# Lookups and pairwise products of a recommendation tower: 16-bit ids, 36 matmuls instead of 40 in a turn, and operands issued in another order

## The chip, the cores and the metric

The kernel runs on one core of a Trainium2 chip. The metric is the device time of one execution in microseconds, as the median of several executions. TensorE is called PE here, VectorE DVE, ScalarE ACT, GpSimd POOL, and SP is the engine that only issues transfers.

## The reference, cut to what matters

```python
def reference(r_bottom_output, ids, tbl_0, ..., tbl_25, W_top1, b_top1, W_top2, b_top2, W_top3):
    e = jnp.stack([tbl_0[ids[:, 0]], tbl_1[ids[:, 1]], ..., tbl_25[ids[:, 25]]], axis=1)   # (512, 26, 128)
    all_emb = jnp.concatenate([r_bottom_output[:, None, :], e], axis=1)                    # (512, 27, 128)
    gram = jnp.einsum('bfd,bgd->bfg', all_emb, all_emb)
    z = gram[:, _TRIU_I, _TRIU_J]                    # the 351 pairs f < g of each sample
    h = jnp.concatenate([z, r_bottom_output], axis=1)                                      # (512, 479)
    h = jnp.maximum(h @ W_top1 + b_top1, 0.0)        # (512, 512)
    h = jnp.maximum(h @ W_top2 + b_top2, 0.0)        # (512, 256)
    return h @ W_top3                                # (512, 1)
```

Everything is fp32. The batch has 512 samples. Nine of the 26 tables have 1000 rows and are looked up in another way than the rest.

## The kernel before, in words

Each engine has its own program, written out by hand in one block, and semaphores tie the programs together. There is no scheduler: the order in the source is the order on the engine.

**Lookups.** Nine tables of 1000 rows (`LOOKED_UP`) are multiplied by one-hot matrices. SP loads a whole table into `tab` (a ring of 3) and the ids of that feature for all 512 samples, broadcast over the partitions, into `hot`. DVE subtracts the first row number of each partition (L351), and makes most of the eight one-hot tiles of 125 x 512 with `is_equal` (L356, `dve_tiles`). ACT makes the rest in two steps, a square (L430) and a relu (L434): one tile in even lookups and two in odd ones. ACT rounds the table to `tab_hi` (L424), DVE subtracts to get `tab_lo` (L297), and PE multiplies both by the one-hots, 8 matmuls each of 512 columns (L661, L666). ACT copies the result into `embT` (L485).

**Gathers.** The other 17 tables are read row by row. POOL issues one indirect DMA for each table and each tile of 128 samples, 68 in all (L284), into `emb`. It starts when `idx`, the ids in sample order, has landed (`s_ids`). The gathered rows are grouped in five banks for each tile (`BANKS`, four features each and one in the last). PE transposes a bank (L535) after its gathers have landed (`s_row[t][i]`) and after an earlier bank has left the same PSUM buffer. Even banks are copied into `embT` by DVE (L294), odd ones by ACT (L412). For tiles 2 and 3 a gather also waits until PE has read the buffer that it overwrites.

**Products.** For each of four tiles of 128 samples, `gram` makes the products of all pairs with 256 small matmuls in the program, in two halves (L549). ACT and DVE copy the halves to `rows` (L217). `turn` (L564) brings them with selection matrices into the layout `products`: for each of four groups of samples it runs over `TURNS`, eight matmuls of three columns of features and two short ones for the last pairs. Then come the layers: high and low parts of the products (L447, L297), layer 1 (L573, L574, L581), relu (L462), transposes of the hidden layer (L622), their high parts (L469) and low parts (L297), and layer 2 and 3 for that tile. The PE program interleaves these stages of neighbouring tiles. The fp32 matmuls of gram and turn appear in the trace as two matmuls each, with a weight load before each of them: 1024 for L549 and 320 for L564.

Two places are touched at the start. SP issues `idx`, waits until it has landed, and then issues the first table's parts, the bottom rows `bot`, the next ids and tables. ACT waits for `s_ids` too before it issues `hot` for the first lookup (L472).

```python
            sp.dma_start(idx[:, :], ids.rearrange("(p t) f -> p (t f)", t=TILES)).then_inc(s_ids, 16)

            sp.wait_ge(s_ids, 16)
            load_table(0, 0, VP_MAIN, 0, VK // 2, s_tab[0])
...
            act.wait_ge(s_ids, 16)
            act.dma_start(hot[:, 0, :], hot_ids[0:1, :].broadcast_to([128, B])).then_inc(s_hotids[0], 16)
```

Of the kernel before, what the change touches and what calls it, by code (L numbers as in the profile page):

```python
# [21 lines left out]
B = 512  # L22
D = 128
TABLES = 26
FEATURES = TABLES + 1
TILES = B // 128
# [4 lines left out]
KTILES = 3  # L31
# [3 lines left out]
         for n in range(8)] + [(range(1, 3), 0, 1, 0, 31), (range(2, 3), 1, 1, 1, 31)]  # L35
LAST_TURN = {j: n for n, (_, _, _, j, _) in enumerate(TURNS)}
# [19 lines left out]
def dve_tiles(i):  # L56

    return VK - 1 - i % 2
# [10 lines left out]
def tower(nc, bottom, ids, hot_ids, tables, w1, w2, b2, w3, out):  # L69
    fp32, fp32r, i32 = mybir.dt.float32, mybir.dt.float32r, mybir.dt.int32  # L70
# [3 lines left out]
    with ctx:  # L74
# [10 lines left out]
        hot = sb("hot", [128, RING, B], i32)  # L85
# [15 lines left out]
        sel = sb("sel", [128, len(TURNS), 4, 32])  # L101
# [126 lines left out]
        def _(sp):  # L228
# [12 lines left out]
            def load_weights(c):  # L241
                sp.wait_ge(s_look, (LOOKED - RING + c // 2 + 1) * VK)
                if c <= KTILES:
                    dst, src = chunk(c), w1[:, c, :]
                else:
                    dst = chunk(c).rearrange("p (k n) -> p k n", n=N2)
                    src = w2.rearrange("(k p) n -> p k n", p=128)[:, 2 * (c - KTILES - 1):2 * (c - KTILES), :]
                sp.dma_start(dst, src).then_inc(s_w[c], 16)

            sp.dma_start(idx[:, :], ids.rearrange("(p t) f -> p (t f)", t=TILES)).then_inc(s_ids, 16)  # L250

            sp.wait_ge(s_ids, 16)
            load_table(0, 0, VP_MAIN, 0, VK // 2, s_tab[0])
            load_table(0, VP_MAIN, VP, 0, VK, s_tab[0])
            load_table(0, 0, VP_MAIN, VK // 2, VK, s_tab0_rest)
            sp.dma_start(bot[:, :, :], bottom.rearrange("(p t) d -> p t d", t=TILES)).then_inc(s_bot, 16)
            load_lookup(1)
# [32 lines left out]
        def _(dve):  # L290
# [49 lines left out]
            nc.vector.memset(sel[:, :, :, :], 0.0).then_inc(s_sel0, 1)  # L340
            dve.wait_ge(s_row0, 1)
            nc.vector.tensor_copy(row0f[:, :], row0[:, :]).then_inc(s_row0f, 1)
            dve.wait_ge(s_sel0, 1)
            dve.wait_ge(s_ident, 1)
            for n, (_, feature, features, j, row) in enumerate(TURNS):
                nc.vector.tensor_copy(sel[:, n, :, row:row + features], ident[:, :].rearrange(
                    "r (s f) -> r s f", f=32)[:, :, feature:feature + features]).then_inc(s_sel, 1)
            dve.wait_ge(s_row0f, 1)
            for i in range(LOOKED):
# [14 lines left out]
                if 2 <= i < 2 + len(BANKS):  # L364
                    copy_bank(0, i - 2)
            low_weights(0, FIRST_CHUNKS)
            for i in range(LOOKED - 2, len(BANKS)):
                copy_bank(0, i)
            copy_bank(1, 1)
            dve.wait_ge(s_bothi, 1)  # L370
            subtract(bot_lo[:, :, :], embT[:, :, :, 0], bot_hi[:, :, :]).then_inc(s_botlo, 1)
# [36 lines left out]
        def _(act):  # L408
# [62 lines left out]
            act.wait_ge(s_ids, 16)  # L471
# [4 lines left out]
            for i in range(LOOKED):  # L476
# [4 lines left out]
                if i == 0:  # L481
# [5 lines left out]
                if 0 < i <= len(BANKS):  # L487
                    copy_bank(0, i - 1)
# [22 lines left out]
            high_products(2)  # L511
            relu(2)
            copy_bank(3, 2)
# [11 lines left out]
        def _(pe):  # L525
# [29 lines left out]
            def turn(t):  # L555
# [28 lines left out]
            def layer1_bottom(t):  # L584
                if t == 0:
                    pe.wait_ge(s_wlo, 1)
                    pe.wait_ge(s_bothi, 1)
                    pe.wait_ge(s_botlo, 1)
                else:
                    pe.wait_ge(s_h1, 2 * t)  # L590
                for psum, cols in h1_parts(t):
# [60 lines left out]
            for i in range(LOOKED):  # L652
# [15 lines left out]
                if i == 0:  # L668
# [5 lines left out]
                elif i <= len(BANKS):  # L674
                    transpose_bank(0, i - 1)
# [114 lines left out]
```

## Time and profile before

| | us |
|---|---|
| median of 3 runs | 115.28 (115.25 to 115.95) |
| the profiled execution's own time | 115.62 |
| its span in the profile | 113.8 |
| PE busy | 92.2 (81% of the span) |
| POOL busy, nearly all of it the issue of gathers | 69.8 (61%) |
| DVE busy | 65.2 (57%) |
| ACT busy | 61.9 (54%) |

The span is the time between the first and the last recorded instruction; 1.8 us of the execution's own time lie around it. The profiled execution took 0.34 us longer than the median. The busy shares are averages over three stages: lookups until about 51 us, then the four tiles, then the tail of the last tile after about 95 us. "Idle ... <-issue" in a row means that the engine waited for nothing that the profile shows.

### The profile page before, as it was taken

Reading aid. Unit: us, or ns where it says so; the run is one execution under the profiler, and the core shown is the slowest. Engines: PE = TensorE matmul, PEld = TensorE weight load, DVE = VectorE, ACT = ScalarE, POOL = GpSimd, SP = SyncE. Lnnn points to the kernel's source line nnn. Section 1 sums busy time; section 2 is a strip of 40 time slices with the busy share of each in tenths; the row PEclk is TensorE's granted clock in tenths of the full one; section 3 lists DMA queues with packets and bytes.
Section 4 is the critical chain, followed back from the end, with each engine's and each line's share of the span. In section 5 each row is a group of like instructions: output and inputs, shape, how many; then the busy total and the mean of one; then the engine's idle time right before and its main releaser. Section 6 shows DMA issues by size and latency. Waiting matters only on the chain.

```text
span 113.8 us, 3965 instructions
## 1 busy us (share of the span) xinstructions
PE 92.2 (81%) x1692; PEld 73.8 (65%) x1692; DVE 65.2 (57%) x166; ACT 61.9 (54%) x90; POOL 69.8 (61%) x75
## 2 busy tenths in 40 slices
PE   0008999998999797997566999999999995886891
PEld 0007776876776584886445867888786884765771
DVE  6429997999999999964924081416303245120221
ACT  0626499999999999979702234254414145100330
POOL 2777777777777777777777777677777730000000
PEclk9999999999999999999998599999999999999999
DMA  0599989999788887367121222122212210000000
GB/s 19 146 312 281 281 185 242 194 245 227 189 256 215 198 261 228 86 232 233 48 53 46 63 58 56 48 52 69 52 46 61 66 46 0 6 6 6 3 0 1
DMA packets 6701, 13.70 MB, mean 120 GB/s; under 512 B 1926, under 2 KB 2567, under 8 KB 6684
## 3 DMA queue, kind: packets, MB, share of 16 engines
q1 hardware_dynamic: 4364, 8.73, 27.8%
q0 software_dynamic: 2176, 4.46, 15.8%
q10 hardware_dynamic: 144, 0.26, 1.0%
q8 instruction: 13, 0.21, 0.8%
q14 instruction: 4, 0.03, 0.1%
HBM read 13.44 MB, written 0.00 MB: 118 GB/s over the span
## 4 chain that ended last, share of the span: by engine, by line
PE 59%; ACT 18%; issue 12%; DMA 6%; DVE 2%; ACTq 0%; DVEq 0%
PE pG L549 10%; PE pG L661 9%; PE pG L564 8%; PE pG L666 8%; PE pH L573 6%; ACT square L430 5%; PE pH L581 5%; ACT onehot L434 5%; DMA hot<-hot_ids 4%; PE pH L574 4%; PE pT L535 4%; ACT tab_hi L424 3%; ACT embT L412 2%; DMA idx<-ids 2%; PE pG L622 1%
## 5 line engine op out<-in xcount | busy, mean ns | idle before, releaser
L284 POOL DMA_INDIRECT emb<-tbl,idx x68 | 69.1, 1015 | 21.8 <-issue 20.4
L661 PE MATMUL pG<-onehot,tab_hi 125*128 125x512 f32 x72 | 21.2, 433 | 11.1 <-DVE onehot L356 8.8
L661 PEld LDWEIGHTS pG<-onehot,tab_hi 125*128 125x128 f32 x72 | 14.0, 202 | 16.1 <-ACT tab_hi L424 8.8
L356 DVE TENSOR_SCALAR onehot<-hot 125x512 fp32r<-125x512 int32 x59 | 21.9, 438 | 0.3
L666 PE MATMUL pG<-onehot,tab_lo 125*128 125x512 f32 x72 | 18.6, 401 | 0.0
L549 PE MATMUL pG<-embT 128*32 128x26 f32 x1024 | 13.2, 194 | 4.4 <-issue 3.3
L549 PEld LDWEIGHTS pG<-embT 128*32 128x32 f32 x1024 | 11.1, 109 | 8.3 <-issue 5.8
L666 PEld LDWEIGHTS pG<-onehot,tab_lo 125*128 125x128 f32 x72 | 14.1, 196 | 3.1
L412 ACT COPY embT<-pT 128x512 f32<-128x512 f32 (+1 forms) x10 | 10.7, 1072 | 9.8 <-PE pT L535 9.8
L297 DVE TENSOR_TENSOR tab_lo<-tab,tab_hi 125x256 fp32r<-125x256 f32 x36 | 12.8, 412 | 0.8 <-ACT tab_hi L424 0.8
L424 ACT CAST tab_hi<-tab 125x1024 fp32r<-125x1024 f32 (+1 forms) x10 | 10.0, 1002 | 5.3 <-DMA tab<-tbl 5.3
L294 DVE COPY embT<-pT 128x512 f32<-128x512 f32 (+1 forms) x10 | 10.3, 1032 | 3.1 <-PE pT L535 3.1
L564 PE MATMUL pG<-rows,sel 128*32 128x96 f32 (+2 forms) x320 | 9.8, 265 | 2.1 <-issue 1.5
L535 PE MATMUL pT<-ident,emb 128*128 128x128 f32 x68 | 10.7, 280 | 0.8 <-ACT embT L412 0.8
L485 ACT COPY embT<-pG 128x512 f32<-128x512 f32 x9 | 10.9, 1209 | 0.7 <-PE pG L666 0.7
L564 PEld LDWEIGHTS pG<-rows,sel 128*32 128x32 f32 x320 | 8.7, 121 | 3.6 <-issue 3.4
L447 ACT CAST prod_hi<-pG 127x384 fp32r<-127x384 f32 (+2 forms) x5 | 2.0, 416 | 15.1 <-PE pG L564 15.1
L434 ACT ACTIVATE onehot<-square,ones 125x512 fp32r<-125x512 f32 x13 | 9.4, 725 | 0.4
L430 ACT ACTIVATE square<-hot,minus_k 125x512 f32<-125x512 int32 x13 | 9.4, 726 | 0.1
L535 PEld LDWEIGHTS pT<-ident,emb 128*128 128x128 f32 x68 | 7.9, 142 | 2.4 <-DMA emb<-tbl,idx 0.8
L217 DVE COPY rows<-pG 128x416 f32<-128x416 f32 x4 | 2.4, 592 | 11.0 <-PE pG L549 11.0
L297 DVE TENSOR_TENSOR prod_lo<-pG,prod_hi 127x384 fp32r<-127x384 f32 (+2 forms) x5 | 2.4, 477 | 10.3 <-ACT prod_hi L447 10.1
(70 smaller groups left out, 95.8 us busy)
## 6 DMA issues: line engine op xcount, KB each, us to landing
tab<-tbl SPq DMA_DIRECT2D x8, 448.0 KB
hot<-hot_ids SPq DMA_DIRECT2D x8, 256.0 KB, 4.4
tab<-w SPq DMA_DIRECT2D x6, 256.0 KB, 3.5
emb<-tbl,idx POOLq DMA_INDIRECT x68, 4.5
tab<-tbl SPq DMA_DIRECT2D x9, 52.0 KB
tab<-tbl SPq DMA_DIRECT2D x2, 224.0 KB, 5.3
hot<-hot_ids ACTq DMA_DIRECT2D x1, 256.0 KB, 5.0
bot<-bottom SPq DMA_DIRECT2D x1, 256.0 KB, 5.3
```

Of the source, the lines that this page charges most:

```text
L284: nc.gpsimd.indirect_dma_start(out=emb[:, t % 2, g - LOOKED - 1, :], out_offset=None, in_=tables[f], in_offset=bass.IndirectOffsetOnAxis(a ...
L297: return nc.vector.tensor_tensor(lo, whole, hi, ALU.subtract)
L356: nc.vector.tensor_scalar(hot_rows(i, k), hot[0:VP, i % RING, :], float(k), None, ALU.is_equal).then_inc(s_hotv, 1)
L412: nc.scalar.copy(bank_slots(t, i), bank(t, i)).then_inc(s_banka, 1)
L424: nc.scalar.copy(tab_hi[:, i % 2, k:k + step, :], tab[0:VP, i % RING, k:k + step, :]).then_inc(s_tabhi, 1)
L430: nc.scalar.activation(square[:, :], hot[0:VP, i % RING, :], ACT.Square, bias=minus_k[:, k - VK + 2:k - VK + 3]).then_inc(s_sq, 1)
L434: nc.scalar.activation(hot_rows(i, k), square[:, :], ACT.Relu, bias=ones[0:VP, 0:1], scale=-1.0).then_inc(s_hota, 1)
L535: last = nc.tensor.transpose(bank(t, i)[:, m, :], emb[:, t % 2, g - LOOKED - 1, :], ident[:, :])
L549: last = nc.tensor.matmul(gram_blocks(t)[32 * s:32 * s + 32, half, i, :], embT_flat[:, first:first + 32], embT[:, t, p, 1:FEATURES], start ...
L564: last = nc.tensor.matmul(products(t)[32 * j:32 * j + 32, 0:len(columns), 32 * s:32 * s + 32], sel[:, n, s, :], rows[:, t % 2, c:c + len(c ...
L661: nc.tensor.matmul(pG[i % 2][:, 0, :], tab_hi[:, i % 2, k, :], hot_rows(i, k), start=(k == 0), stop=False)
L666: nc.tensor.matmul(pG[i % 2][:, 0, :], tab_lo[:, i % 2, k, :], hot_rows(i, k), start=False, stop=(k == VK - 1)).then_inc(s_look, 1)
```

## The change

Ids for the lookups are sent as 16-bit integers. DVE makes seven one-hot tiles in every lookup, and ACT one. A turn ends with one matmul of 64 output rows instead of two short ones of 32. The first table's parts and the first lookup's ids no longer wait until `idx` has landed. The bottom rows are loaded behind the second lookup's operands, and their transposes and the banks of tile 0 move one lookup later. The second layer's weights are loaded only after the first tile's gram. The low part of the bottom rows is made tile by tile. In tile 2, bank 2 is transposed and copied ahead of layer 1 and the relu.

```diff
-         for n in range(8)] + [(range(1, 3), 0, 1, 0, 31), (range(2, 3), 1, 1, 1, 31)]
-LAST_TURN = {j: n for n, (_, _, _, j, _) in enumerate(TURNS)}
+         for n in range(8)] + [(range(1, 3), 0, 1, 0, 31), (range(1, 3), 1, 1, 1, 31)]
+
+SINGLES = len(TURNS) - 2
+LAST_TURN = {2: 5, 3: 4}
 def dve_tiles(i):
-    return VK - 1 - i % 2
+    return VK - 1
-        hot = sb("hot", [128, RING, B], i32)
+        hot = sb("hot", [128, RING, B], i16)
...
             def load_weights(c):
                 sp.wait_ge(s_look, (LOOKED - RING + c // 2 + 1) * VK)
+                if c == KTILES + 1:
+                    sp.wait_ge(s_gram, 2)
...
             sp.dma_start(idx[:, :], ids.rearrange("(p t) f -> p (t f)", t=TILES)).then_inc(s_ids, 16)
-            sp.wait_ge(s_ids, 16)
             load_table(0, 0, VP_MAIN, 0, VK // 2, s_tab[0])
             load_table(0, VP_MAIN, VP, 0, VK, s_tab[0])
+            sp.wait_ge(s_ids, 16)
             load_table(0, 0, VP_MAIN, VK // 2, VK, s_tab0_rest)
+            load_lookup(1)
             sp.dma_start(bot[:, :, :], bottom.rearrange("(p t) d -> p t d", t=TILES)).then_inc(s_bot, 16)
-            load_lookup(1)
             load_lookup(2)
...
-                if 2 <= i < 2 + len(BANKS):
-                    copy_bank(0, i - 2)
+                if 3 <= i < 3 + len(BANKS):
+                    copy_bank(0, i - 3)
...
-            subtract(bot_lo[:, :, :], embT[:, :, :, 0], bot_hi[:, :, :]).then_inc(s_botlo, 1)
+            for t in range(TILES):
+                subtract(bot_lo[:, t, :], embT[:, t, :, 0], bot_hi[:, t, :]).then_inc(s_botlo, 1)
...
-            act.wait_ge(s_ids, 16)
             act.dma_start(hot[:, 0, :], hot_ids[0:1, :].broadcast_to([128, B])).then_inc(s_hotids[0], 16)
...
             high_products(2)
+            copy_bank(3, 2)
             relu(2)
-            copy_bank(3, 2)
             high_h1(2)
...
                 for s in range(4):
-                    for n, (columns, _, _, j, row) in enumerate(TURNS):
+                    for n, (columns, _, _, j, row) in enumerate(TURNS[:SINGLES]):
                         c = columns[0] - 1
-                        last = nc.tensor.matmul(products(t)[32 * j:32 * j + 32, 0:len(columns), 32 * s:32 * s + 32],
-                                                sel[:, n, s, :], rows[:, t % 2, c:c + len(columns), :],
-                                                start=row == 0, stop=LAST_TURN[j] == n)
+                        nc.tensor.matmul(products(t)[32 * j:32 * j + 32, 0:len(columns), 32 * s:32 * s + 32],
+                                         sel[:, n, s, :], rows[:, t % 2, c:c + len(columns), :],
+                                         start=row == 0, stop=LAST_TURN.get(j) == n)
+                    last = nc.tensor.matmul(products(t)[0:64, 0:2, 32 * s:32 * s + 32], single[:, s, :],
+                                            rows[:, t % 2, 0:2, :], start=False, stop=True)
...
-                if i == 0:
+                if i == 1:
                     pe.wait_ge(s_ident, 1)
                     pe.wait_ge(s_bot, 16)
...
             transpose_bank(3, 1)
+            transpose_bank(3, 2)
             layer1_high(2, whole)
             layer1_low(2, whole)
-            transpose_bank(3, 2)
             transpose_bank(3, 3)
             transpose_h1(2)
             transpose_bank(3, 4)
...
-    arrays["hot_ids"] = ids.reshape(128, TILES, TABLES).transpose(2, 1, 0)[LOOKED_UP].reshape(LOOKED, B)
+    arrays["hot_ids"] = ids.view(np.int16)[:, ::2].reshape(128, TILES, TABLES).transpose(2, 1, 0)[LOOKED_UP].reshape(LOOKED, B)
```

The first transfers that SP issues, before (the row of 112x512 after the 13x1024 row is the table's second half; L256 is `bot`; the wait for `idx` stands behind the first DMA):

```order
L250 DMA idx<-ids 128x104
L231 DMA tab<-tbl_3 112x512
L231 DMA tab<-tbl_3 13x1024
L231 DMA tab<-tbl_3 112x512
L256 DMA bot<-bottom 128x512
L237 DMA hot<-hot_ids 128x512
L231 DMA tab<-tbl_4 112x1024
L231 DMA tab<-tbl_4 13x1024
```

And in the changed kernel, where the wait stands behind the 13x1024 row:

```order
L256 DMA idx<-ids 128x104
L234 DMA tab<-tbl_3 112x512
L234 DMA tab<-tbl_3 13x1024
L234 DMA tab<-tbl_3 112x512
L240 DMA hot<-hot_ids 128x512
L234 DMA tab<-tbl_4 112x1024
L234 DMA tab<-tbl_4 13x1024
L263 DMA bot<-bottom 128x512
```

The bottom rows moved behind the second lookup's three transfers, and two table transfers moved ahead of the wait.

PE around the last banks of tile 3, before. `pT0<-ident,emb` is the transpose of an even bank, `pT1<-ident,emb` that of an odd one, and `pG0<-ident,h1` the transpose of the hidden layer of tile 2. Behind the last row stand the transpose of bank 4 and tile 3's gram:

```order
L564 MATMUL pG0<-rows,sel 32x32
L535 MATMUL pT0<-ident,emb 128x128 x4
L573 MATMUL pH1<-w_hi,prod_hi 128x512
L574 MATMUL pH1<-w_lo,prod_hi 128x512
L573 MATMUL pH1<-w_hi,prod_hi 128x512
L574 MATMUL pH1<-w_lo,prod_hi 128x512
L573 MATMUL pH1<-w_hi,prod_hi 128x512
L574 MATMUL pH1<-w_lo,prod_hi 128x512
L581 MATMUL pH1<-w_hi,prod_lo 128x512 x3
L535 MATMUL pT1<-ident,emb 128x128 x4
L535 MATMUL pT0<-ident,emb 128x128 x4
L622 MATMUL pG0<-ident,h1 128x128 x4
```

The same stretch in the changed kernel:

```order
L543 MATMUL pT0<-ident,emb 128x128 x4
L543 MATMUL pT1<-ident,emb 128x128 x4
L583 MATMUL pH1<-w_hi,prod_hi 128x512
L584 MATMUL pH1<-w_lo,prod_hi 128x512
L583 MATMUL pH1<-w_hi,prod_hi 128x512
L584 MATMUL pH1<-w_lo,prod_hi 128x512
L583 MATMUL pH1<-w_hi,prod_hi 128x512
L584 MATMUL pH1<-w_lo,prod_hi 128x512
L591 MATMUL pH1<-w_hi,prod_lo 128x512 x3
L543 MATMUL pT0<-ident,emb 128x128 x4
L632 MATMUL pG0<-ident,h1 128x128 x4
L543 MATMUL pT1<-ident,emb 128x128
```

The odd bank's transposes moved ahead of layer 1, and what follows layer 1 is only the even bank (bank 3), the hidden layer and bank 4.

The last turn on PE, before:

```order
L581 MATMUL pT1<-w_hi,bot_lo 128x256
L564 MATMUL pG1<-rows,sel 32x3x32 x8
L564 MATMUL pG1<-rows,sel 32x2x32
L564 MATMUL pG1<-rows,sel 32x32
L564 MATMUL pG1<-rows,sel 32x3x32 x8
L564 MATMUL pG1<-rows,sel 32x2x32
L564 MATMUL pG1<-rows,sel 32x32
```

And in the changed kernel:

```order
L591 MATMUL pT1<-w_hi,bot_lo 128x256
L572 MATMUL pG1<-rows,sel 32x3x32 x8
L575 MATMUL pG1<-rows,single 64x2x32
L572 MATMUL pG1<-rows,sel 32x3x32 x8
L575 MATMUL pG1<-rows,single 64x2x32
```

Each group of samples has 9 matmuls in the program instead of 10, and a turn, which has four groups, 36 instead of 40.

## Rows read from the trace of the kernel before

**Rows 1.** The waits of all engines: engine, line, releaser, us in total, times, longest.
```profile
POOL emb L284 <- issue: 20.4, 67, 0.3
PEld pT L535 <- DMA emb<-tbl,idx: 0.8, 1, 0.8
```
**Rows 2.** The timeline of POOL: start, duration, instruction, idle before it.
```profile
2.90 1.11 POOL L284 DMA_INDIRECT emb<-tbl,idx  x1 [1.34 <-DMA idx<-ids]
...
32.69 1.09 POOL L284 DMA_INDIRECT emb<-tbl,idx  x1 [0.30 <-issue]
...
54.40 1.46 POOL L284 DMA_INDIRECT emb<-tbl,idx  x1 [0.30 <-issue]
...
91.45 0.94 POOL L284 DMA_INDIRECT emb<-tbl,idx  x1 [0.31 <-issue]
```
**Rows 3.** The tile `emb`, its gathers from issue to landing.
```profile
DMA to landing us min/median/max: 2.5/4.5/7.3
```
**Rows 4.** The timeline of all engines around the last gather's landing.
```profile
92.55 1.04 PE L535 MATMUL pT<-ident,emb 128*128 128x128 f32 x8
...
93.29 1.18 ACT L412 COPY embT<-pT 128x512 f32<-128x512 f32 x1
...
94.21 0.74 ACT L469 CAST h1T_hi<-pG 128x256 fp32r<-128x256 f32 x2
94.58 0.14 PEld L535 LDWEIGHTS pT<-ident,emb 128*128 128x128 f32 x1 [0.80 <-DMA emb<-tbl,idx]
...
94.94 0.41 ACT L412 COPY embT<-pT 128x128 f32<-128x128 f32 x1
```
**Rows 5.** The timeline of PE's matmuls in the tail.
```profile
95.50 1.36 PE L549 MATMUL pG<-embT 128*32 128x26 f32 x128 [0.59 <-ACT embT L412]
...
98.85 0.28 PE L549 MATMUL pG<-embT 128*32 128x26 f32 x9
99.50 1.21 PE L549 MATMUL pG<-embT 128*32 128x26 f32 x119 [0.38 <-issue]
...
101.54 0.35 PE L564 MATMUL pG<-rows,sel 128*32 128x96 f32 x2
103.39 1.83 PE L564 MATMUL pG<-rows,sel 128*32 128x96 f32 x78 [1.50 <-issue]
```
**Rows 6.** The same view in the gram of tile 0.
```profile
56.46 0.74 PE L549 MATMUL pG<-embT 128*32 128x26 f32 x63 [1.36 <-issue]
...
58.02 0.72 PE L549 MATMUL pG<-embT 128*32 128x26 f32 x61
60.29 0.25 PE L549 MATMUL pG<-embT 128*32 128x26 f32 x3 [1.56 <-issue]
```
**Rows 7.** The page's DMA queues: packets, MB, share; and its line of PE instructions.
```profile
PE 92.2 (81%) x1692; PEld 73.8 (65%) x1692; DVE 65.2 (57%) x166; ACT 61.9 (54%) x90; POOL 69.8 (61%) x75
...
q8 instruction: 13, 0.21, 0.8%
```
**Rows 8.** The chain that ended last, its first steps: start, us, what.
```profile
0.74 1.89 DMA idx<-ids
...
2.65 4.98 DMA hot<-hot_ids
```
**Rows 9.** The groups by form on DVE: busy us, mean ns.
```profile
L356 DVE TENSOR_SCALAR onehot<-hot 125x512 fp32r<-125x512 int32 x59 | 21.9, 438 | 0.3
...
L297 DVE TENSOR_TENSOR tab_lo<-tab,tab_hi 125x256 fp32r<-125x256 f32 x36 | 12.8, 412 | 0.8 <-ACT tab_hi L424 0.8
...
L297 DVE TENSOR_TENSOR bot_lo<-embT,bot_hi 128x512 fp32r<-128x512 f32 x1 | 1.2, 1189 | 1.2 <-ACT bot_hi L491 1.2
```
**Rows 10.** Busy time by stretch: its length, engines with instruction counts, PEclk, DMA share, GB/s.
```profile
8.20:48.90 40.70, 37.78 (x158) 29.21 (x159) 39.52 (x107) 37.55 (x48) 31.64 (x30) 1.00 0.87 221
...
54.90:61.50 6.60, 3.16 (x142) 2.33 (x145) 3.14 (x7) 2.45 (x5) 5.08 (x6) 1.00 0.19 49
61.50:64.90 3.40, 3.40 (x81) 3.23 (x74) 0.69 (x1) 0.23 (x2) 2.50 (x3) 0.50 0.23 63
```

More of the change, by code:

```diff
@@ L69, in tower @@
 def tower(nc, bottom, ids, hot_ids, tables, w1, w2, b2, w3, out):
-    fp32, fp32r, i32 = mybir.dt.float32, mybir.dt.float32r, mybir.dt.int32
+    fp32, fp32r, i32, i16 = mybir.dt.float32, mybir.dt.float32r, mybir.dt.int32, mybir.dt.int16
     ALU, ACT = mybir.AluOpType, mybir.ActivationFunctionType
@@ L100, in tower @@
         bot_lo = sb("bot_lo", [128, TILES, 128], fp32r)
-        sel = sb("sel", [128, len(TURNS), 4, 32])
+        sel = sb("sel", [128, SINGLES, 4, 32])
+        single = sb("single", [128, 4, 64])
         rows = sb("rows", [128, 2, COLS, GROUPS])
@@ L340, in _ @@
             nc.vector.memset(sel[:, :, :, :], 0.0).then_inc(s_sel0, 1)
+            nc.vector.memset(single[:, :, :], 0.0).then_inc(s_sel0, 1)
             dve.wait_ge(s_row0, 1)
             nc.vector.tensor_copy(row0f[:, :], row0[:, :]).then_inc(s_row0f, 1)
-            dve.wait_ge(s_sel0, 1)
+            dve.wait_ge(s_sel0, 2)
             dve.wait_ge(s_ident, 1)
             for n, (_, feature, features, j, row) in enumerate(TURNS):
-                nc.vector.tensor_copy(sel[:, n, :, row:row + features], ident[:, :].rearrange(
+                to = sel[:, n, :, row:row + features] if n < SINGLES else single[:, :, 32 * j + row:32 * j + row + 1]
+                nc.vector.tensor_copy(to, ident[:, :].rearrange(
                     "r (s f) -> r s f", f=32)[:, :, feature:feature + features]).then_inc(s_sel, 1)
@@ L363, in _ @@
                              tab_hi[:, i % 2, ks, :]).then_inc(s_tablo, 1)
-                if 2 <= i < 2 + len(BANKS):
-                    copy_bank(0, i - 2)
+                if 3 <= i < 3 + len(BANKS):
+                    copy_bank(0, i - 3)
             low_weights(0, FIRST_CHUNKS)
-            for i in range(LOOKED - 2, len(BANKS)):
+            for i in range(LOOKED - 3, len(BANKS)):
                 copy_bank(0, i)
@@ L486, in _ @@
                     "d (t p) -> d t p", p=128)).then_inc(s_lookc, 1)
-                if 0 < i <= len(BANKS):
-                    copy_bank(0, i - 1)
+                if 1 < i <= 1 + len(BANKS):
+                    copy_bank(0, i - 2)
             copy_bank(1, 0)
@@ L587, in layer1_bottom @@
                     pe.wait_ge(s_bothi, 1)
-                    pe.wait_ge(s_botlo, 1)
                 else:
                     pe.wait_ge(s_h1, 2 * t)
+                pe.wait_ge(s_botlo, t + 1)
                 for psum, cols in h1_parts(t):
@@ L667, in _ @@
                                      start=False, stop=(k == VK - 1)).then_inc(s_look, 1)
-                if i == 0:
+                if i == 1:
                     pe.wait_ge(s_ident, 1)
@@ L673, in _ @@
                     last.then_inc(s_bank, 1)
-                elif i <= len(BANKS):
-                    transpose_bank(0, i - 1)
+                elif 1 < i <= 1 + len(BANKS):
+                    transpose_bank(0, i - 2)
             transpose_bank(1, 0)
```

## The prediction

> **What bounds the kernel now.** I read the waits first. POOL's gathers are the longest entry, 20.4 us in 67 pieces of at most 0.3 us, and none of it is a wait for another engine [rows 1]. The timeline of POOL says the same: the first gather starts at 2.90, just after `idx` has landed, and the last of the 68 at 91.45 [rows 2]. The stream never stops. Whatever PE, DVE and ACT do earlier, the last gather can't be issued sooner unless the stream starts sooner or its steps get shorter. A quiet gather takes 0.94 to 0.95 us plus 0.30 of issue; beside DVE work it takes 1.09, and once 1.46.
>
> The second question is whether the end hangs on this stream. A gather lands at the earliest 2.5 us after its issue [rows 3], so the last one lands at 93.95. PE's transpose of it starts at 94.58 [rows 4]. The weight load names the gather as its releaser, but ACT's copy of bank 2, which frees the same PSUM buffer, runs from 93.29 to 94.47 and is the later of the two. The slack between the two theories is only 0.6 us: gain more than that on PE and ACT, and the gathers are the bound.
>
> The third is the tail, from the gram of tile 3 at 95.50 to the end. There PE stands still for 1.50 us in the middle of the last turn, 2 matmuls in, where no instruction waits for anything [rows 5]. The same happens for 1.36 and 1.56 us in tile 0's gram [rows 6]. I count what lies between. From 56.46 to 60.29 there are 63 + 61 gram matmuls and 3 of layer 1, so 127 matmuls, each with its weight load: 254 instructions and a few waits. From 99.50 to 103.39 there are 119 + 6 + 2 = 127 as well. The page has 13 instruction transfers of 0.21 MB together, 16 KB each, for some 3,400 PE instructions [rows 7], or about 260 each. So these are the edges of blocks of 256 instructions, and a block that is used up faster than the next one arrives costs a stall. The edges are 3.83 us apart there, and 3.89 in the tail. Counting 127 matmuls back from 99.50 (9, then 14 of layer 2, then 104) puts the edge before it 24 matmuls into the gram, at 95.75: 3.75 us. About 3.8 us is the price of a block in this kernel when PE wants it sooner.
>
> **The change, part by part.** The sum is made against the profiled execution's own 115.62 us (span 113.8 and 1.8 around it). That execution took 0.34 us more than the median; its PE clock fell to half from 61.5 to 64.9 [rows 10], behind a stretch in which PE was busy for 3.16 of 6.60 us, and a late PE is part of what I count as gain below.
>
> *Start of the lookups.* The first ids land 4.98 us after an issue at 2.65, and that issue had waited for `idx` [rows 8]. It now comes 1.9 us sooner. In the lookups DVE is busy for 39.52 of 40.70 us [rows 10], so it sets their pace. It gets 4 more one-hots at 21.9/59 = 0.37 us: +1.5. The subtraction of the ids on 16 bits may get cheaper or not. ACT loses 4 squares and relus, in cover of DVE. So the lookups end 0.4 to 1.9 us sooner. Worth at the end: 0, because the gathers cover it. The moved bottom rows, banks of tile 0 and copies cost 0 for the same reason; they lie 70 us ahead of the stream's end, with none of their gathers late.
>
> *Start of the gathers.* `idx` used to travel alone, 1.89 us. Now two table transfers follow it on SP's queue and 128 KB of ids go out on ACT's at the same moment. Below, the cost is 0: `idx` is issued first. Above, it lands as late as the ids do beside the table, 4.98 us after issue: +3.1. I take +0.15, near the lower end, since the others are issued behind it or at best with it and `idx` is small (128 x 104 ids of 4 bytes, 52 KB). SP's wait for `idx` now stands behind two transfers (0.8 us of issue) and ahead of the table's second half; `idx` lands later than those are issued, so nothing queued behind it is delayed.
>
> *Steps of the gathers.* In the lookups 30 gathers take 31.64 us [rows 10], 0.11 each above the quiet 0.945, 3.3 us in all beside 39.5 us of DVE. The 1.5 us of added DVE work cost 1.5 x 3.3/39.5 = 0.12. The gather beside the single `bot_lo` subtraction, 1189 ns [rows 9], took 1.46, 0.51 above quiet; four short ones in its place save between 0 and 0.5. I put the sum of both at 0, with -0.5 and +1.5 (every added microsecond paid in full) as ends. The Trainium skill, GPSIMD Engine Reference, § Specifications, says that GpSimd shares its SBUF interfaces with VectorE and contends with DVE instructions of two SBUF inputs or in a two-port mode. The trace fits that, 1.46 beside a subtraction of two SBUF tensors.
>
> *From the last gathers to the gram of tile 3.* Bank 2 is now transposed and copied before layer 1 and the relu of tile 2, so ACT's copy is out of the way. The last gather of bank 3 is issued one step of 1.25 before 91.45 and lands at 92.70. PE, which reached it at about 93.0 before (eight transposes from 92.55, 0.11 apart), is now there sooner and waits. Then: four transposes until 93.15, four of the hidden layer until 93.60, ACT's high parts 0.74 to 94.35, its copy of bank 4 0.41 to 94.76, and 0.14 of issue, as before [rows 4]. The gram starts at 94.90 instead of 95.50: -0.60. The last gather itself allows this: landed 93.95, transposed 94.25, ahead of ACT. If PE in a median execution is already early, 0.3 of it is missing.
>
> *The turn.* Nine matmuls instead of ten in each of four groups, two passes each: 72 in place of 80. At 1.83/78 = 23.5 ns [rows 5] that is 0.19 us a turn. Turns 0 to 2 are covered by the gathers. The larger effect is the edges. Ahead of the last gram stand 48 instructions less and 2 waits more (the low bottom part of tiles 1 and 2), so each edge comes 23 matmuls later in the program: the first 47 matmuls into the gram instead of 24, 0.50 us after its start instead of 0.25. The next two edges follow at the price of blocks, at 0.50 + 3.75 = 4.25 and 4.25 + 3.89 = 8.14 us (before 7.89). The third then lies about 25 matmuls into the last turn instead of 2, and leaves 72 - 25 = 47 behind it instead of 78: 1.10 us in place of 1.83. The turn ends at 9.24 instead of 9.72 us behind the gram's start: -0.48. The new matmul of 64 output rows is in no row; the nearest are the two that it replaces, so it costs between one of them (0) and both (8 x 0.0235 = 0.19). I take 0.03.
>
> Here a page stands against the row. The Trainium skill, Runtime: NRT & Kernel Launch, § Instruction fetch mechanics, says that the crossing of a 16 KiB boundary is "mostly hidden". By it the edges cost nothing and the turn gives 0.19. The trace shows 1.50 us on the path, so the sum goes by the row.
>
> *Second layer's weights.* SP now holds them until tile 0's gram is done. Behind that wait stands only the output. At up to 5 us to land [rows 8] they may reach ACT 1 us late; it falls in tile 0 and 1, where the gathers cover it.
>
> The sum: +0.15 + 0 - 0.60 - 0.45 = -0.90, so 115.62 - 0.90 = **114.7 us**, 0.5% below the median. A difference of 1% is about what a measurement of this kernel can tell from none, so the forecast is within 1%.
>
> **Rivals.** *The ids come late (slower).* `idx` shares the transfer engines with two parts of the table and the first ids. Its price is the delay itself, all on the path, because the stream has no slack: up to 3.1 us, so up to 117.7. At 1.05 us late the change is even with the median, from 2.2 us it is slower by 1%. For it speaks that ids beside a table took 4.98 us; against it, that `idx` is ahead in its queue. I take 117 for its middle; chance 0.09.
>
> *The one-hot tiles run at half speed with a 16-bit source (slower).* Now 512 elements take 371 ns, while a two-input subtraction takes 12.8/36 = 356 for 256 [rows 9]. No row has mixed widths. At the second rate a tile costs 0.27 us more (256 elements of some 1.04 ns), 63 tiles 17 us, far beyond the cover of 2 us: about 129. The Trainium skill, VectorE: DVE Perf Modes, § What auto-detection actually checks, ties the two-port mode to SBUF operands and even sizes, not to 16 bits, and so speaks against it. Chance 0.04.
>
> *A lull lowers PE's clock.* PE arrives at bank 3 up to 2 us early and idles until 92.7, then works for 0.9 and idles again until 94.9. After the stretch of 3.16 busy us in 6.60 the clock fell for 3.4 us and the 80 matmuls of a turn took 3.40 in place of 80 x 0.0235 = 1.88 [rows 5, 10]. In the tail such a fall costs 1.5 us at most, and about 0.8 where PE waits for blocks anyway: 115.5. Chance 0.15.
>
> *More is gained.* The gathers' steps get shorter by the quarter subtractions, or blocks arrive at 3.5 instead of 3.8 us apart (-0.6): 113.9. Chance 0.18.
>
> *Nothing is gained,* since a median execution already waits for the gathers and the edges fall as badly as before: 115.2. Chance 0.12.
>
> **How the numbers follow.** The forecast has 0.42, and its own range is 114.1 to 115.3. Faster by over 1% (below 114.13): 0.18 and a quarter of the forecast's lower half, 0.06, so 0.24. Slower by over 1% (above 116.43): late ids 0.07, the slow one-hots 0.04, and a clock fall at full price together with dearer gathers 0.04, so 0.15. Within: 0.61. The range reaches from 113.7 to 116.6 and leaves out the slow one-hots and the far ends of the late ids and of the gain.
>
> **What would show it.** In the profile after, the first gather should start at 2.9 to 3.2, the last at about 91.6. The first lookup should start 1.9 us sooner, and the lookups end 0.4 to 1.9 us sooner. PE should wait for a gather before bank 3, and the gram of tile 3 start 1.0 us after the last gather has landed. The stall in the last turn should stand 25 matmuls in. The prediction is wrong if the gather stream starts or runs otherwise by over 1 us, if one-hots don't take 0.37 us, or if the stalls in the tail move in another way than by the count of instructions.

## The result

The changed kernel takes **116.47 us** (median of 4 runs, 116.08 to 117.8) against 115.27 us for the kernel before (113.91 to 115.95) on the same chip: ratio 1.018, interval 1.011 to 1.025. It is slower by 1.2 us where 0.6 us less was forecast. Every ratio here leaves out, on both sides, the executions that took over 1.5% longer than the fastest of the same kernel, so it isn't always the ratio of the two medians beside it.

The profiled execution took 116.64 us, span 114.8, against 115.62 and 113.8. First the gather stream, POOL's timeline (start, duration, instruction, idle before it):

```profile
4.63 1.11 POOL L290 DMA_INDIRECT emb<-tbl,idx  x1 [3.07 <-DMA idx<-ids]
...
92.76 0.94 POOL L290 DMA_INDIRECT emb<-tbl,idx  x1 [0.30 <-issue]
```

The stream starts 1.73 us later than in [rows 2] and ends 1.31 later. The chain that ended last begins with the reason, and SP's queue shows the third table transfer held up by it:

```profile
0.74 3.61 DMA idx<-ids
4.63 1.11 POOL emb L290
```
```profile
0.74 0.39 ACTq L480 DMA_DIRECT2D hot<-hot_ids  x1
0.74 0.39 SPq L256 DMA_DIRECT2D idx<-ids  x1
1.19 3.50 SPq L234 DMA_DIRECT2D tab<-tbl  x3
```

`idx` is issued at 0.74 as before and takes 3.61 us instead of 1.89 [rows 8]. The waits (engine, line, releaser, us in total, times, longest) say that the stream itself still stops for nothing:

```profile
POOL emb L290 <- issue: 19.8, 65, 0.3
```

Between the last gather and the end, PE's timeline of matmuls:

```profile
94.04 0.66 PE L543 MATMUL pT<-ident,emb 128*128 128x128 f32 x4 [2.19 <-DMA emb<-tbl,idx]
...
96.26 1.84 PE L557 MATMUL pG<-embT 128*32 128x26 f32 x128 [0.60 <-ACT embT L421]
...
102.97 0.54 PE L572 MATMUL pG<-rows,sel 128*32 128x96 f32 x16
103.43 0.33 PE L575 MATMUL pG<-rows,single 128*64 128x64 f32 x2
103.69 0.37 PE L572 MATMUL pG<-rows,sel 128*32 128x96 f32 x7
104.40 0.44 PE L572 MATMUL pG<-rows,sel 128*32 128x96 f32 x9 [0.34 <-issue]
104.76 0.33 PE L575 MATMUL pG<-rows,single 128*64 128x64 f32 x2
105.02 0.54 PE L572 MATMUL pG<-rows,sel 128*32 128x96 f32 x16
105.49 0.33 PE L575 MATMUL pG<-rows,single 128*64 128x64 f32 x2
105.75 0.54 PE L572 MATMUL pG<-rows,sel 128*32 128x96 f32 x16
106.21 0.33 PE L575 MATMUL pG<-rows,single 128*64 128x64 f32 x2
```

Here gram(3) is the gram of tile 3, and a pass is one of the two matmuls that the trace has for each fp32 matmul of the program (a gram is 128 matmuls in the program and 256 passes). An edge is the end of a block of 256 instructions, as the prediction counted them. Three things are to be seen. PE now waits for the gathers before bank 3, for 2.19 us, and gram(3) starts 3.50 us behind the last gather's issue (before 4.05). The edge in the last turn stands 16 + 2 + 7 = 25 passes in. And a group of 16 + 2 passes, which the turn repeats four times, takes 105.75 - 105.02 = 0.73 us, of which the two passes of the 64-row matmul take 105.75 - 105.49 = 0.26. A group of the old turn took 20 x 0.0235 = 0.47 [rows 5].

The clock was lower in one stretch of the tail (columns as in [rows 10]):

```profile
96.40:100.00 3.60, 3.60 (x136) 3.32 (x131) 0.08 (x1) 0.51 (x1) 0.00 (x0) 0.53 0.03 7
100.00:114.00 14.00, 11.52 (x250) 9.33 (x249) 2.93 (x9) 2.03 (x6) 0.00 (x0) 1.00 0.01 2
```

So the 1.0 us more of span is +1.31 at the last gather, -0.55 from there to gram(3), +0.55 from gram(3) to the turn's end (10.28 us against 9.73), and -0.31 behind it (8.28 against 8.59). The +0.55 is the clock's: gram(3)'s first half took 1.84 us instead of 1.36 [rows 5], and in another profile of the changed kernel, at full clock in this stretch, the turn ends 9.76 us behind gram(3)'s start (experiment 11).

### The profile page after: what moved, and what is told of

Same layout as the page of the kernel before. It is cut to its first block, busy times and chain, and to the rows that moved or that the text cites. A ratio compares the mean times of both kernels' runs of the same rounds, so it can differ in the third digit from the quotient of the medians.

```text
span 114.8 us, 3901 instructions
## 1 busy us (share of the span) xinstructions
PE 96.9 (84%) x1660; PEld 74.8 (65%) x1660; DVE 65.0 (57%) x174; ACT 57.1 (50%) x82; POOL 69.4 (60%) x75
## 4 chain that ended last, share of the span: by engine, by line
POOL 42%; PE 29%; issue 16%; DMA 8%; POOLq 1%; ACT 1%; DVE 1%; ACTq 0%; DVEq 0%
POOL emb L290 42%; PE pG L557 7%; PE pG L572 5%; DMA emb<-tbl,idx 5%; PE pH L583 4%; DMA idx<-ids 3%; PE pG L575 3%; PE pH L584 2%; PE pH L591 2%; PE pT L543 2%; POOLq L76 1%; PE pG L632 1%; PE pH L643 1%; DVE rows L220 1%; PE pT L584 0%
## 5 line engine op out<-in xcount | busy, mean ns | idle before, releaser
L671 PE MATMUL pG<-onehot,tab_hi 125*128 125x512 f32 x72 | 22.1, 446 | 6.8 <-ACT tab_hi L433 6.8
L364 DVE TENSOR_SCALAR onehot<-hot 125x512 fp32r<-125x512 int16 x63 | 22.6, 428 | 0.3
L557 PE MATMUL pG<-embT 128*32 128x26 f32 x1024 | 13.7, 198 | 3.1 <-issue 2.0
L557 PEld LDWEIGHTS pG<-embT 128*32 128x32 f32 x1024 | 11.7, 114 | 6.9 <-issue 4.5
L572 PE MATMUL pG<-rows,sel 128*32 128x96 f32 x256 | 9.2, 253 | 1.0 <-DVE rows L220 0.5
L572 PEld LDWEIGHTS pG<-rows,sel 128*32 128x32 f32 x256 | 5.4, 109 | 3.3 <-issue 2.3
L439 ACT ACTIVATE square<-hot,minus_k 125x512 f32<-125x512 int16 x9 | 6.5, 728 | 1.2 <-DVE hot L359 1.2
L443 ACT ACTIVATE onehot<-square,ones 125x512 fp32r<-125x512 f32 x9 | 6.5, 725 | 0.3
```

What stands on the lines that cost most here:

```text
L364: nc.vector.tensor_scalar(hot_rows(i, k), hot[0:VP, i % RING, :], float(k), None, ALU.is_equal).then_inc(s_hotv, 1)
L557: last = nc.tensor.matmul(gram_blocks(t)[32 * s:32 * s + 32, half, i, :], embT_flat[:, first:first + 32], embT[:, t, p, 1:FEATURES], start ...
L671: nc.tensor.matmul(pG[i % 2][:, 0, :], tab_hi[:, i % 2, k, :], hot_rows(i, k), start=(k == 0), stop=False)
```

## The experiments

Each ratio is to runs of the kernel before on the same chip. Experiments 1 to 4 ran on one chip, 5 to 8 on a second and 9 to 12 on a third, where the kernel before was at 115.64, 115.56 and 114.70 us. Differences between chips are therefore read from profiles.

**1. Both waits for `idx` back** (`e1_both_wait`), the rest as changed.

```diff
             sp.dma_start(idx[:, :], ...).then_inc(s_ids, 16)
+            sp.wait_ge(s_ids, 16)
             load_table(0, 0, VP_MAIN, 0, VK // 2, s_tab[0])
             load_table(0, VP_MAIN, VP, 0, VK, s_tab[0])
-
-            sp.wait_ge(s_ids, 16)
...
+            act.wait_ge(s_ids, 16)
             act.dma_start(hot[:, 0, :], ...)
```

> The changed kernel with both waits for the ids put back: the first table and the first lookup's ids go out only when idx has landed. Theory 1 (late ids: in the changed kernel idx landed 3.61 us after its issue instead of 1.89, and the first gather started at 4.63 instead of 2.90): the first gather starts at 2.9 and the last at 91.1, 1.7 us sooner than in the changed kernel (92.76), so the time falls by 1.3 to 1.7 us, to about 114.9, at or a little below the kernel before. Theory 2 (the loss is TensorE's clock, which fell to half from 96.6 to 100.0 in the tail because TensorE now idles before the last gathers): the stream moves, but the lull stays, and the time falls by under 0.5 us, to 116 or more.

Measured 114.18 us against 115.64: ratio 0.989 (0.982 to 0.996). The first gather starts at 2.98, the last at 90.38, and gram(3) at 93.84, 3.46 behind it. The late ids are what makes the changed kernel slow; without them the rest is a gain of 1%.

The last gather comes 2.38 us sooner than in the changed kernel, and only 1.65 of that is the start. From the first gather to the last it is 87.40 us here and 88.13 in the changed kernel. In the kernel before it is 88.55, but 87.75 in experiment 9, whose lookups are the same. So the steps of the gathers differ by 0.8 us between profiles without a change to them, and whether the 0.73 us belong to the late ids stays open.

**2. and 3. One wait each.** `e2_tables_wait` has SP's wait alone back (ACT's ids go out at once), `e3_hot_waits` ACT's alone (the table follows `idx` at once).

> The changed kernel with only SP's wait put back, ahead of the first table; ACT still issues the first lookup's ids (128 KB) at once. Theory 1a (any transfer beside idx delays it, the ids on ACT's queue most, since they start in the same microsecond): idx lands 2.5 to 3.3 us after its issue and most of the loss stays, about 115.8. Theory 1b (the table in the same queue is what delays it): idx lands after about 2.0 us, and the time is that of the version with both waits.

> The changed kernel with only ACT's wait put back; the two table transfers still follow idx at once in SP's queue. Theory 1a: idx lands after about 2.0 us, since the table is queued behind it, and the time is that of the version with both waits, about 114.9. Theory 1b: it lands 2.5 to 3.3 us after its issue and most of the loss stays.

The start of each chain, of `e2_tables_wait` and then of `e3_hot_waits`:

```profile
0.74 3.21 DMA idx<-ids
4.23 1.11 POOL emb L289
```
```profile
0.74 1.83 DMA idx<-ids
2.59 3.49 DMA hot<-hot_ids
```

The ids on ACT's queue do nearly all of it: 1.006 (1.001 to 1.011) with them beside `idx`, 0.994 (0.990 to 0.997) with only the table behind it. Two table transfers behind `idx` on its own queue cost nothing by themselves (1.83 us to land, 1.89 before). Beside the ids they add 0.2 to 0.4 us (3.41, 3.53 and 3.61 in three profiles with both, 3.21 with the ids alone). The Trainium skill, DMA: Bandwidth & Descriptors, § Queues, rings and completion order, says that each DMA engine takes turns between the queues that have work, packet by packet. The first part of this agrees: a transfer behind `idx` on the same queue doesn't slow it (1.83 us), one on another queue does (3.21). Whether the engines take turns packet by packet no run here shows.

**4. The same in the kernel before** (`e4_start_only`): both waits moved as in the change, nothing else.

> The kernel before with nothing changed but the start: both waits for the ids taken away (the first two table transfers ahead of SP's wait, no wait on ACT), ids still 32 bits wide, 256 KB on ACT's queue. Theory 1: the gathers start at least 1.7 us later (the ids beside idx are twice as large), and the kernel before becomes slower by 1.3 to 2.3 us, about 117, though its lookups start sooner. Theory 2: the start alone costs under 0.5 us.

Measured 117.4 against 115.64 us, ratio 1.015 (1.009 to 1.020). `idx` takes 4.92 us there and the first gather starts at 5.93: with ids of 32 bits ACT's transfer has 256 KB instead of 128, and delays `idx` by 3.0 us instead of 1.7. The 16-bit ids halve the harm that their early issue does.

```profile
0.74 4.92 DMA idx<-ids
```

**5. Experiment 1 with the old turn** (`e5_old_turn`).

```diff
-         for n in range(8)] + [(range(1, 3), 0, 1, 0, 31), (range(1, 3), 1, 1, 1, 31)]
-SINGLES = len(TURNS) - 2
-LAST_TURN = {2: 5, 3: 4}
+         for n in range(8)] + [(range(1, 3), 0, 1, 0, 31), (range(2, 3), 1, 1, 1, 31)]
+SINGLES = len(TURNS)
+LAST_TURN = {j: n for n, (_, _, _, j, _) in enumerate(TURNS)}
...
-                    last = nc.tensor.matmul(products(t)[0:64, 0:2, 32 * s:32 * s + 32], single[:, s, :],
-                                            rows[:, t % 2, 0:2, :], start=False, stop=True)
```

> The version with both waits put back (e1), and with the old turn of 40 matmuls. In e1 the turn of tile 3 ended 9.70 us behind the start of tile 3's gram. Theory 1 (block edges every 256 instructions set the pace there): the edges move 24 matmuls forward in the program again, the third falls a few matmuls into the last turn with some 78 left, and the turn ends about 0.5 us later, at 10.1 to 10.2; the time rises by 0.4 to 0.6 us. Theory 2 (only the work counts): it rises by 0.19 us.

Measured 113.78 against 115.56 us, ratio 0.993 (0.989 to 0.997). Experiment 1 had 0.989 (0.982 to 0.996) on another chip, so the runs show neither the 0.4 to 0.6 us that the count of edges forecast nor a gain. The profiles say more. In PE's timeline the 79 passes behind the edge take 1.87 us, and the stall stands at the turn's start:

```profile
99.60 0.27 PE L572 MATMUL pG<-rows,sel 128*32 128x96 f32 x1
101.20 1.87 PE L572 MATMUL pG<-rows,sel 128*32 128x96 f32 x79 [1.32 <-issue]
```

From gram(3) to the turn's end it takes 9.41 us, in experiment 1 9.70, with this stall:

```profile
101.40 0.43 PE L572 MATMUL pG<-rows,sel 128*32 128x96 f32 x9 [0.97 <-issue]
```

The new turn moves the edge to a better place and loses at least that by its own length.

**6. Experiment 1 with bank 2 back behind layer 1 and the relu** (`e6_old_bank2`).

```diff
-            copy_bank(3, 2)
             relu(2)
+            copy_bank(3, 2)
...
-            transpose_bank(3, 2)
             layer1_high(2, whole)
             layer1_low(2, whole)
+            transpose_bank(3, 2)
```

> e1 with bank 2 of tile 3 again transposed and copied behind layer 1 and the relu of tile 2. Theory 1 (TensorE comes early to the last banks and waits for the gathers): nothing changes, because ACT copies bank 2 before the last gather lands; the gram of tile 3 still starts 3.4 to 3.5 us after the issue of the last gather (e1: 3.46), and the time stays within 0.2 us. Theory 2 (the move of bank 2 was what shortened it from the 4.05 us of the kernel before): it starts 4.0 us after, and the time rises by 0.5 us.

Measured 114.86 against 115.56 us, ratio 0.999 (0.991 to 1.006). Its profile, with the clock lower from 94.3, has gram(3) 3.41 us behind the last gather, as near as with the bank moved:

```profile
92.80 0.66 PE L543 MATMUL pT<-ident,emb 128*128 128x128 f32 x4 [1.93 <-DMA emb<-tbl,idx]
...
94.91 1.92 PE L557 MATMUL pG<-embT 128*32 128x26 f32 x128 [0.59 <-ACT embT L420]
```

Once PE is early, it waits for the gathers in either order, and moving bank 2 is worth nothing that the profile shows. The ratio doesn't contradict this, nor does it prove it: 0.999 and experiment 1's 0.989 come from two chips, and their intervals overlap.

**7. Work for PE in the wait** (`e8_filler`): experiment 1 with 9 matmuls of 512 columns ahead of bank 3, into the second layer's accumulator, which is started anew behind them.

> e1 with 9 more matmuls of 512 columns (2.1 us, into an unused half of a PSUM tile's bank, their result is overwritten) between tile 2's layer 1 and the transposes of bank 3, where TensorE waits for a gather for 2.2 us in the changed kernel. Theory 1 (in some executions the lull lowers the clock in the tail, at 0.5 to 1 us each): the granted clock shows no low stretch after 90 us in any execution, and the median falls by 0.2 to 0.5 us although work was added. Theory 2 (the clock costs nothing there, since the blocks of instructions set the pace): the median stays or rises by up to 0.3 us.

Measured 115.95 against 115.56 us, ratio 1.006 (0.999 to 1.013). In the profile, of an execution of 117.87 us, gram(3) starts 4.68 us behind the last gather instead of 3.46, and the clock fell all the same, from 104.3 to 111.1. Of the 12 executions 5 had a mean clock of 1.0 and 6 one of 0.967 to 0.971. Filling the wait doesn't keep the clock up here, and it delays bank 3.

**8. Edges moved by padding** (`e9_edges`): experiment 1 with 32 small matmuls (64 passes) in the same place, all into rows 0 to 31.

```diff
+                pe.wait_ge(s_y, 2)
+                for _ in range(matmuls):
+                    nc.tensor.matmul(pH2[0:32, 0:COLS], embT_flat[:, 0:32], embT[:, 0, 0, 1:FEATURES],
+                                     start=True, stop=True)
```

> e1 with 32 added fp32 matmuls of 32 x 26 outputs (128 instructions, some 0.7 us) at the same place ahead of bank 3's transposes, into a PSUM tile whose content is overwritten later. They only move the edges: one then falls at their end, inside the wait for the gathers. Theory 1 (edges 3.8 us apart at least): the next falls about 110 matmuls into tile 3's gram, which is reached at +1.2 us, the next near the end of the second half at about +5.0, and the one after that lies behind the turn. The turn ends 7.8 to 8.2 us behind the start of the gram instead of 9.70, with no stall inside it, and the time falls by 1.2 to 1.8 us, to about 112.8. Theory 2 (the stall in the turn has another cause, a wait that the profile doesn't show): no gain, or 0.1 us slower.

Measured 115.28 against 115.56 us, ratio 1.002 (0.995 to 1.008). The padding and what follows, in PE's timeline:

```profile
90.97 2.21 PE L567 MATMUL pH<-embT 128*32 128x26 f32 x64
93.11 0.66 PE L543 MATMUL pT<-ident,emb 128*128 128x128 f32 x4
...
99.66 0.46 PE L557 MATMUL pG<-embT 128*32 128x26 f32 x32 [0.26 <-issue]
```

The edges moved by count: the one in gram(3)'s second half stands 96 passes in, where it would be 32 without the 64 of the padding. The last turn has no stall, and ends 8.81 us behind gram(3)'s start instead of 9.70. But 64 passes in one column group (a column group here is the set of 32 output rows, out of 128, that a matmul writes) took 2.21 us, where the gram's 64, which rotate over four groups, take 0.7. They delayed bank 3, and gram(3) came 1.3 us later, which cancelled the gain.

**9. The new turn alone, in the kernel before** (`e11_new_turn`). The diff is the one of experiment 5 the other way round, with the tile `single`.

> The kernel before with the new turn alone (36 matmuls with the one 64-row matmul a pass in place of 40). Theory 1, the 64-row matmul costs about 0.13 us in each of its 8 passes where the ones it replaces cost 0.0235: every group of one slice takes 0.73 us, the turn 2.9 us of PE time against 1.9, and in the last turn, which is on the path, that is 0.8 to 1.0 us more, less what a shifted block edge gives; total 115.6 to 116.4 against 115.5. Theory 2, the matmuls saved are worth their edges and the wide one is free, as the prediction had it: 0.4 to 0.6 us faster, 114.9 to 115.1, and a last turn whose passes stay 0.0235 us apart.

Measured 119.42 against 114.70 us, ratio **1.039** (1.033 to 1.046), far beyond what either theory gave (0.8 to 1.0 us more, or 0.5 less). Its gathers are as good as before (2.87 to 90.62). gram(3) starts 9.08 us behind the last one, where it was 4.05. No wait stands between tile 2's turn and gram(3) except ACT's last copies:

```profile
92.40 0.54 PE L569 MATMUL pG<-rows,sel 128*32 128x96 f32 x16
92.87 0.33 PE L572 MATMUL pG<-rows,single 128*64 128x64 f32 x2
93.12 0.54 PE L569 MATMUL pG<-rows,sel 128*32 128x96 f32 x16
93.59 0.33 PE L572 MATMUL pG<-rows,single 128*64 128x64 f32 x2
93.85 0.66 PE L540 MATMUL pT<-ident,emb 128*128 128x128 f32 x4
...
96.75 1.04 PE L540 MATMUL pT<-ident,emb 128*128 128x128 f32 x8
97.62 0.60 PE L629 MATMUL pG<-ident,h 128*128 128x128 f32 x4
98.81 0.30 PE L540 MATMUL pT<-ident,emb 128*128 128x128 f32 x1 [0.59 <-ACT embT L417]
99.70 1.28 PE L554 MATMUL pG<-embT 128*32 128x26 f32 x128 [0.59 <-ACT embT L417]
```

From tile 2's turn to gram(3) it is 99.70 - 93.92 = 5.78 us, and 95.50 - 89.72 = 5.78 in the kernel before. So PE sets the time there in both, and what the first three turns take arrives at the end. They take 4.33 + 3.40 + 3.39 us, before 3.41 + 2.02 + 2.27: +3.4 of the 4.2 us by which tile 2's turn ends later. The other 0.8 weren't followed up. In the kernel before this work had no cover.

In the changed kernel it has. There the last of the lookups' low matmuls starts at 46.57 instead of 50.26, and tile 2's turn ends at 88.03, ahead of 89.72 in spite of the longer turns; the 2.19 us of waiting at bank 3 are what is left.

The earlier start is the smaller part of these 3.7 us. In experiment 1, where the lookups wait for `idx` again, that matmul starts at 47.73. So 2.5 us come from the other edits to the lookups, and 1.2 from the start. In the kernel before, the chain that ended last runs over ACT's squares and relus in the lookups, and PE waited for the second tile that ACT made:

```profile
44.70 0.47 PE L661 MATMUL pG<-onehot,tab_hi 125*128 125x512 f32 x1 [0.69 <-ACT onehot L434]
```

The changed kernel has no such wait for `onehot` from ACT. That the tile taken from ACT gave most of the 2.5 us fits this; no run has that edit alone.

**10. and 11. The changed kernel with the old turn** (`e13_after_old_turn`), **and itself again** (`e14_after_again`) as its partner.

> The changed kernel with the old turn of 40 matmuls, all else as changed. Theory 1 (the new turn costs more than it saves): 0.2 to 0.8 us faster than the changed kernel on the same chip, about 115.9; turn back at 1.9 us of PE time with one stall of about 1.3 us at its start. Theory 2: about 0.5 us slower than the changed kernel.

> The changed kernel itself once more, so that the run with the old turn has a partner on its own chip: 116.1 to 116.7, ratio 1.005 to 1.012 to the kernel before, of which the late ids are +1.3 us at the stream's end, and the rest of the tail is even.

Measured 116.19 (ratio 1.016, 1.010 to 1.022) and 115.93 us (1.013, 1.007 to 1.019): no difference that can be measured. The profiles, first the last turn of `e13_after_old_turn`, then the end of that of `e14_after_again`:

```profile
102.20 0.27 PE L572 MATMUL pG<-rows,sel 128*32 128x96 f32 x1
103.52 1.87 PE L572 MATMUL pG<-rows,sel 128*32 128x96 f32 x79 [1.05 <-issue]
```
```profile
103.72 0.43 PE L572 MATMUL pG<-rows,sel 128*32 128x96 f32 x9 [0.69 <-issue]
```

In `e14_after_again` the clock was full over this stretch (1.00 from 94 on). The turn ends 9.76 us behind gram(3)'s start; the edge comes 7.61 us behind it (8.14 forecast), and the 47 passes left take 2.15 us (1.10 forecast). In `e13_after_old_turn` it ends after 9.00 us. The profile favours the old turn by 0.76 us and the medians don't; the runs of the old turn had the lower granted clocks (0.955 to 0.984 against 0.956 to 1.0), and whether that hides a gain stays open. One profile of each says little. Over all that have full clock in this stretch, the old turn ends 9.00 to 9.73 us behind gram(3)'s start (four: the kernel before and experiments 4, 5 and 10) and the new one 9.45 to 9.98 (five: experiments 1, 2, 3, 9 and 11).

**12. Experiment 5 with 16 small matmuls over four column groups** (`e12_best_pad`).

> The version with both waits on the ids put back and the old turn, and 16 gram-shaped matmuls (four column groups in turn, 64 records of the block of 256) between layer 1 of tile 2 and the bank of the 23rd to 26th features of tile 3, where PE waits for a gather anyway. They write into the second layer's accumulator, which is started anew behind them, so the output is the same. Theory of the block edges: the edge that fell on gram(3)'s first instruction moves into the wait, the next two come 64 records earlier, so the stall of 1.3 us at the last turn's start falls to 0.3 to 0.7 us: 112.8 to 113.3 against 113.78. Rival, the edges come at the pace of the blocks' arrival and are only moved, or the pad delays the bank behind it as the 32 one-group matmuls did: 113.8 to 114.6.

Measured 116.31 against 114.70 us, ratio 1.014 (1.008 to 1.020): the rival, and worse. The stall in the turn is gone, but the last gather is late:

```profile
90.78 0.45 PE L568 MATMUL pH<-embT 128*32 128x26 f32 x32
91.90 0.65 PE L543 MATMUL pT<-ident,emb 128*128 128x128 f32 x4 [0.67 <-DMA emb<-tbl,idx]
...
94.29 0.33 PE L543 MATMUL pT<-ident,emb 128*128 128x128 f32 x1 [1.30 <-DMA emb<-tbl,idx]
...
103.14 1.95 PE L580 MATMUL pG<-rows,sel 128*32 128x96 f32 x80
```
```profile
q0 software_dynamic: 31, 0.07, 15.7%
q8 instruction: 1, 0.02, 5.1%
```

The second fence is the DMA view of 91.8 to 93.3: one instruction packet of 16 KB, busy for 5.1% of 16 engines x 1.5 us = 1.2 us. `e5_old_turn` has no such packet between its last gather's issue and landing. The last gather, issued at 90.66, lands 3.6 us later instead of 2.5. The edge was moved into PE's wait, and the fetch fell on the last gather. The other traces bear this out: in the 14 profiles, 25 gathers issued after 60 us took 2.81 to 4.34 us to land, and each of them had such a packet in flight while it was under way. But about as many met one and landed within 2.75 us, among them the last gather of experiment 9 (2.5 us, the packet began 0.35 before it landed). So a fetch can delay a gather and needn't. The clock was lower too, from 94.8 to 101.6, so the 1.1 us of the gather are only part of the loss.

## Why the prediction was wrong

The sum was -0.90 us, and the profile gives +1.0. The prediction had named this as a sign of being wrong: a gather stream that starts otherwise by over 1 us. By its steps:

- **Start of the gathers: the first term that was mis-sized.** Forecast +0.15, measured +1.73 at the first gather. I had the bound right (+3.1) and chose the lower end, because `idx` stood ahead in its queue. That argument holds for its own queue alone, as experiment 3 shows, and not for ACT's (experiment 2). The nearest row was the ids' own 4.98 us beside the table [rows 8], a transfer beside one on another queue, and I set it aside. The rival "the ids come late", with a chance of 0.09, had this mechanism, and its point from which it decides, 1.05 us, was passed. (That point is reckoned from the profiled execution's 115.62 us; against the median of 115.28 it is 0.71 us, and 1.86 instead of 2.2 for 1%.)
- **Steps of the gathers: right in size.** Forecast 0 (-0.5 to +1.5), measured -0.42 at the last gather, 1.31 late instead of 1.73. This is less than the 0.8 us by which two profiles with the same lookups differ (experiment 1), so it shows neither a gain nor a loss.
- **From the last gather to gram(3): right.** 3.50 us, forecast 3.45. But experiment 6 says that the bank's move didn't bring it; PE's earliness did.
- **The turn: the second term that was mis-sized.** The 64-row matmul was costed at 0.03 us, at most 0.19. It takes 0.13 us a pass, 1.04 in its 8 passes, and the old group of 20 passes at 0.47 us became one of 18 at 0.73. At full clock the turn ends 9.76 us behind gram(3)'s start where 9.24 was forecast and 9.73 measured before: the gain of 0.45 is gone. I had priced it by the matmuls that it replaces, though these overlap with their neighbours in other column groups: it was a new shape of instruction and no row bounded it from above. The Trainium skill, TensorEngine Tiling (Array Packing), § Key Properties, says that changing the tiling mode drains TensorE. The runs agree in kind: the passes of 32 rows run 0.029 us apart between two of the wide ones, each of which takes 0.13. That it is a drain, and not the two groups being occupied together, no run here tells apart.
- **The edges: right.** The count was exact, 25 matmuls into the turn. The stall was smaller than before (0.34 and 0.69 us in two profiles of the changed kernel, 0.97 in experiment 1). In the one at full clock the edge came 0.5 us sooner than forecast, and the longer turn reached it later.
- **Lookups earlier, "worth 0": wrong, and hidden in the sum.** They gave PE the 3.7 us that paid for three longer turns. Experiment 9 shows the price without them: +4.7 us. The forecast of 0.4 to 1.9 us was too small as well, because it took DVE for the engine that sets the lookups' pace. The chain of the kernel before runs over ACT's squares and relus there, and ACT is the engine that the change relieved. "The gathers cover it" was written of each edit by itself, while the kernel before had no cover on PE at all: its 5.78 us from turn to gram are PE's own, and PE was already 0.6 us late.
- **The one-hots with 16-bit ids:** 63 of them take 428 ns on average (438 before) and 22.6 us in all, 0.36 each (0.37 before); that rival is refuted. **The clock's lull** happened in the profile, and there it cost the 0.55 us between gram(3) and the turn's end. But the execution at full clock still took 116.31, so it isn't the cause.

The 1.8% are thus in the main the ids, +1.3 us at the end of the stream against this profile of the kernel before and +2.4 against experiment 1's. The turn's length took back what the better edge gave, and the sooner gram's 0.55 us were too little to cover the ids. How the microseconds divide is known no better than this, since the stream itself varies by 0.8 us between profiles. Experiments 1 and 5 are faster than both kernels, 0.989 and 0.993 of the kernel before; which turn is the better one there, on one chip, wasn't measured.

## What to carry to other kernels

A small load that a long stream waits for should have the DMA engines to itself: being first in its own queue doesn't protect it from a transfer on another. When matmuls are merged to save instructions, count what ran side by side before, and take a new output shape as unpriced until a row shows it. "Covered" is a statement about a budget that all edits share: sum the added work of each engine against the slack of that engine, not each edit against the bound.

## What the runs showed of the hardware

- A matmul over 64 output rows amid ones of 32 rows takes 0.13 us a pass, where the 32-row ones of 96 columns take 0.0235 to 0.029 in four column groups in turn. Passes of 26 columns take 0.010 (1.28/128) in four groups in turn and 0.034 (2.21/64) when all are in one.
- 128 KB on another queue delay a transfer of 52 KB by 1.3 us alone and by 1.5 to 1.7 with a table behind it; 256 KB with a table by 3.0.
- An instruction block of 16 KB arrives as one packet on one DMA engine, 1.2 us in experiment 12. The last gather there met it and landed 1.1 us late, while that of experiment 9 met one and landed in the usual 2.5 us.
